# A memory layer with half of its heads multiplied in full: four dense heads and four gathered ones, in 64 slots, with every engine's order planned anew

## The reference

```python
# 1 token mixer: 4 x 4 pixels are pooled into each of 256 tokens by an attention with 8 heads
h1 = mean_of_patch + softmax(q @ k) @ v @ proj_w.T + proj_b
# 2 Mamba-like mixer on layernorm(h1): two selective scans over 256 tokens, 128 channels x 16 states
h2 = h1 + (concat(y_forward * silu(z), y_backward * silu(z)) * gate) @ W_out.T
# 3 product-key memory on layernorm(h2)
q = (x @ Wq_pk).reshape(b, n, 2, 8, 32).transpose(2, 0, 1, 3, 4)
sim = einsum('pbnhd,pkhd->pbnhk', q, pk_keys)      # 2 sides, 8 heads, 64 keys each
scores, idx = top_k(sim, 16)                       # 16 of each side
score = scores[0][..., :, None] + scores[1][..., None, :]
final_scores, pk_idx = top_k(score, 16)            # 16 of the pairs: rows of a table of 4096 per head
weights = softmax(final_scores)
# each token and head: weighted sum of 16 rows of keys_table and values_table,
# then causal attention of each head over the 256 tokens, and Wo
```

## Time and profile before

| | |
|---|---|
| median of 3 runs | 13356.86 us (13354.56 to 13362.06) |
| profiled execution | 13354.71 us, its span 13352.6 us |
| TensorE busy (weight loads) | 11719.0 us, 88% (9286.1 us, 70%) |
| VectorE, ScalarE, POOL busy | 78%, 55%, 77% |
| mean granted TensorE clock | 0.933 |
| indirect DMAs | 9216, 1108 ns each |
| slots | 3584, 56 per image |

### The profile page before, as it was taken

One profiled execution on the slowest core, in us unless ns is written; L12 is line 12 of the kernel. 1 busy time (PEld: TensorE's weight loads), 2 busy tenths in 40 slices (PEclk: granted clock), 3 DMA queues, 4 the chain that ended last, 5 costly groups with the idle time before them and its releaser, 6 DMA issues.

```text
span 13352.6 us, 262103 instructions
## 1 busy us (share of the span) xinstructions
PE 11719.0 (88%) x71396; PEld 9286.1 (70%) x71396; DVE 10428.1 (78%) x39940; ACT 7363.4 (55%) x17030; POOL 10215.8 (77%) x9220
## 2 busy tenths in 40 slices
PE   3888888988989889989889888898888888898988
PEld 3677677776777767777767677776677677776776
DVE  7878778778778787787777877877878878778772
ACT  2555555555555555555555555555555555555554
POOL 1777777777777777777777777777777777777776
PEclk6999999999999999999999999999999999999999
DMA  2555555555555555555555555555555555555554
GB/s 73 160 145 153 157 145 154 154 144 159 145 151 158 144 154 153 147 156 148 149 159 146 151 159 143 155 154 146 157 143 153 159 145 153 158 142 157 152 140 120
DMA packets 1668219, 1983.98 MB, mean 149 GB/s; under 512 B 532846, under 2 KB 1134062, under 8 KB 1666286
## 3 DMA queue, kind: packets, MB, share of 16 engines
q1 hardware_dynamic: 1371566, 1359.71, 35.8%
q0 software_dynamic: 294912, 604.57, 17.5%
HBM read 1898.00 MB, written 65.01 MB: 147 GB/s over the span
## 4 chain that ended last, share of the span: by engine, by line
PE 38%; DVE 26%; POOL 18%; issue 11%; DMA 4%; ACT 2%; SPq 0%; DVEq 0%; POOLq 0%; ACTq 0%
POOL gath L801 18%; PE bank L991 9%; PE bank L1032 6%; PE bank L873 4%; PE bank L1019 3%; DVE apart L1701 3%; PE bank L1006 3%; DVE row_f L1704 3%; DMA gath<-in_table_dram,rowsT 2%; DVE decay L1576 2%; PE bank L954 2%; DVE onehot L1803 2%; PE bank L977 2%; PE bank L1050 1%; DMA moving<-keyspace 1%
## 5 line engine op out<-in xcount | busy, mean ns | idle before, releaser
L801 POOL DMA_INDIRECT gath<-in_table_dram,rowsT x9216 | 10215.6, 1108 | 3105.9 <-issue 2673.7
L1256 ACT ACTIVATE weight<-bank 128x512 f32<-128x512 f32 x3584 | 2139.3, 597 | 4415.0 <-PE bank L1006 4383.9
L991 PE MATMUL bank<-weight,rowtab 128*128 128x256 f32 x12288 | 3373.8, 399 | 0.0
L1032 PEld LDWEIGHTS bank<-spread,gath 128*128 128x128 f32 x18432 | 2519.7, 201 | 727.8 <-DMA gath<-in_table_dram,rowsT 607.6
L1032 PE MATMUL bank<-spread,gath 128*128 128x96 f32 x18432 | 2524.3, 282 | 519.0 <-DMA gath<-in_table_dram,rowsT 518.8
L991 PEld LDWEIGHTS bank<-weight,rowtab 128*128 128x128 f32 x12288 | 2460.7, 202 | 620.3 <-issue 102.2
L1249 ACT ACTIVATE bank<-bank,seventeen 128x512 f32<-128x512 f32 x3584 | 2370.6, 661 | 13.3 <-PE bank L1006 10.2
L1019 PE MATMUL bank<-moving,pick_b 96*128 96x512 bf16 x3584 | 1457.5, 407 | 304.7 <-ACT bank L1249 226.5
L1006 PE MATMUL bank<-moving,pick_b 96*128 96x512 bf16 x3584 | 1435.0, 400 | 71.1 <-DMA moving<-keyspace 70.6
L1568 DVE TENSOR_TENSOR_SCAN decay<-decay,wide 128x1024 f32<-128x1024 f32 x512 | 1169.3, 2285 | 26.4
L1836 DVE SCALAR_TENSOR_TENSOR acc<-bank,rrow,acc 128x64 f32<-128x64 f32 x1024 | 240.5, 276 | 839.3 <-PE bank L1006 797.2
(11 more groups left out here) (268 smaller groups left out, 18929.9 us busy)
## 6 DMA issues: line engine op xcount, KB each, us to landing
rowtab<-in_tableD_dram SPq DMA_DIRECT2D x2048, 256.0 KB
wide<-states SPq DMA_DIRECT2D x512, 512.0 KB
moving<-keyspace SPq DMA_DIRECT2D x3072, 64.0 KB
gath<-in_table_dram,rowsT POOLq DMA_INDIRECT x9216
pix<-in_x_dram SPq DMA_DIRECT2D x504, 256.0 KB
moving<-keyspace SPq DMA_DIRECT2D x3072, 32.0 KB
keyspace<-split SPq DMA_DIRECT2D x192, 256.0 KB, 2.1
moving<-keyhalf SPq DMA_DIRECT2D x512, 64.0 KB
```

Of the source, the lines that this page charges most:

```text
L801: pool.indirect_dma_start(out=gath[:, u % RING, j, :], out_offset=None, in_=table, in_offset=bass.IndirectOffsetOnAxis(ap=rowsT[k][:, col: ...
L991: mm(dense_ps[:, 0:TOK], rowtab[:, r, s % 2 * 2 + half, :], weight[s % 2][:, half * TOK:(half + 1) * TOK], start=(s % 16 == 0 and half == ...
L1032: mm(sums_ps[:, col:col + STREAM], gath[:, u % RING, j, :], flat[:, col:col + STREAM], start=True, stop=True)
L1256: ins = af(weight[s % 2][:], zd_ps[s % 2][:], ACT.Exp, scale=-1.0)
```

## The change

Head 3 becomes dense for all its tokens, and heads 4 to 7 are gathered. The image has 64 full slots in place of 48 full and 8 half ones, 128 gathers in 32 parts in place of 144 in 36, and eight `S.R` in place of ten. The ring of gathered parts has 4 places in place of 6. The table tiles stay 32 per image, the key rows go from 56 loads to 64. The second logarithm `l2`, `selh`, `X5`, `wb4`, `k4` and `K3`'s half go; `split_h` and `keyhalf` are replaced by a fourth full set in `split` and `keyspace`. VectorE's `L` lists work on 8 units in place of 6 and its `G` lists on 8 in place of 10. All four order strings are written anew. `pr0` and `A0` now wait for the `T` lists.

```diff
-DENSE = 3
+DENSE = 4
-HU = DU + TILES
+HU = DU
-SLOTS = 16 * DENSE + 8
+SLOTS = 16 * DENSE
-PARTS = (GH * SPAN - SPAN // 2) // PART
-RING = 6
+PARTS = GH * SPAN // PART
+RING = 4
...
 PE_ORDER = """
...
-21 z20+0 a0.6+0 o21+0 d19+0 g1.5+0 a1.0+0
-22 z21+0 o22+0 d20+0
...
-55 z54+0 o55+0 d53+0 S.E2+1 F.y+2
+1 z0+0 d63-1 o1+0 g0.0+0 a5.6-1 S.A3+0 F.g+1
...
+25 z24+0 o25+0 d23+0 g1.4+0 a0.6+0
+26 z25+0 o26+0 d24+0 a1.0+0
...
+39 z38+0 o39+0 d37+0 g2.3+0 a2.5+0 F.xd+2 F.dt+2
+40 z39+0 o40+0 d38+0
+41 z40+0 o41+0 d39+0 g2.4+0 a2.6+0 S.E0+1
+42 z41+0 o42+0 d40+0 a3.0+0
...
+63 z62+0 o63+0 d61+0 g3.7+0 a5.5+0 S.E2+1 F.y+2
...
 ACT_ORDER = """
...
+0 w63-1 l0+0 k3-1 a5.5-1 F.sq2+2 F.sq3+2 S.E2+0
...
 DVE_ORDER = """
...
+5 a6.3-1 S.n0+1 S.n1+1 S.lo3+0 S.R7+0
...
+40 S.e0+1 S.pr1+1
+41 S.e1+1
+42 F.dl+2 a2.5+0 S.R0+1 a2.6+0
+43 S.e2+1 S.e3+1 F.B0+2
+44 
+45 S.R1+1 F.sf0+2
+46 S.R2+1 a3.3+0
+47 F.sb0+2 F.B1+2 S.lo1+1
+48 F.sf1+2
+49 F.sb1+2 a3.5+0
+50 F.B2+2 a3.6+0 S.e4+1
+51 F.sf2+2 F.C0+2
+52 
+53 F.sb2+2 a4.3+0 F.B3+2
+54 F.C1+2 F.sf3+2
+55 a4.5+0 F.sb3+2
+56 a4.6+0 S.A2+1
+57 F.C2+2 S.wh+1 S.re2+1
+58 S.A3+1 F.C3+2
+59 S.R3+1 a5.3+0
+60 
+61 S.wb0+1 S.e5+1 a5.5+0
+62 S.R4+1 S.lo2+1 S.R5+1
+63 S.wb1+1 S.R6+1
...
 SP_ORDER = """
...
-35 bc+2 m38+0
...
-42 lq0+2 t23+0 m45+0
-43 m46+0
-44 lq1+2 t24+0 m47+0
...
+16 t10+0 x0+3 m19+0
...
+37 x1+3 m40+0
...
+40 t22+0 bc+2 m43+0
...
+48 t26+0 x2+3 m51+0
+49 m52+0
+50 lq1+2 lq0+2 t27+0 m53+0
+51 m54+0
+52 t28+0 st0+1 m55+0
+53 m56+0
+54 x3+3 t29+0 m57+0
+55 m58+0
+56 lq2+2 t30+0 m59+0
+57 m60+0
+58 x4+3 x5+3 st1+1 t31+0 lq3+2 m61+0
+59 x6+3 m62+0
...
+64 x7+3
...
-                if h < DENSE:
-                    mm(dense_ps[:, 0:TOK], rowtab[:, r, s % 2 * 2 + half, :],
...
-                else:
-                    for q in (2 * half, 2 * half + 1):
-                        mm(dense_ps[:, 0:P], rowtab[:, r, q, :], weight[s % 2][:, q * P:(q + 1) * P],
-                           start=(s % 16 == 0 and q == 0), stop=(s == SLOTS - 1 and q == 3),
-                           skip_group_check=True)
+                mm(dense_ps[:, 0:TOK], rowtab[:, r, s % 2 * 2 + half, :],
+                   weight[s % 2][:, half * TOK:(half + 1) * TOK],
+                   start=(s % 16 == 0 and half == 0), stop=(s % 16 == 15 and half == 1),
+                   skip_group_check=True)
```

More of the change, by code:

```diff
@@ L195 @@
+45 w44+0 l45+0 F.dc2+2
+46 w45+0 l46+0 a3.4+0
+47 w46+0 l47+0 F.dc3+2
+48 w47+0 l48+0 k2+0 F.dc4+2 a3.5+0 K2+0
+49 w48+0 l49+0
+50 w49+0 l50+0 F.dc5+2 S.E1+1
+51 w50+0 l51+0 a4.0+0
+52 w51+0 l52+0 S.wg+1
+53 w52+0 l53+0 F.dc6+2
+54 w53+0 l54+0 F.dc7+2
+55 w54+0 a4.4+0 l55+0
+56 w55+0 a4.5+0 l56+0
+57 w56+0 l57+0
+58 w57+0 l58+0 S.hi2+1
+59 w58+0 l59+0 a5.0+0
+60 w59+0 l60+0
+61 w60+0 l61+0
+62 w61+0 l62+0 a5.4+0
+63 w62+0 l63+0 S.mi2+1
 """
 DVE_ORDER = """
-0 a5.6-1 F.y+1 F.ps+2
-1 S.R9+0 S.e6+0
@@ L249 @@
[L249 to L253, removed]
+0 F.y+1 a5.6-1
+1 F.ps+2 F.g+1
+2 S.e6+0 S.e7+0
+3 F.h2+1 S.re3+0
+4
+5 a6.3-1 S.n0+1 S.n1+1 S.lo3+0 S.R7+0
+6 F.rf+2 a6.5-1
+7 a6.6-1 S.T0+1
+8
+9
+10 S.T1+1 S.T2+1 S.T3+1
+11 S.T5+1 S.T4+1
+12
+13 S.T6+1 S.T7+1 a7.3-1
+14 S.T10+1
+15 S.T8+1 S.T9+1 F.var+2 S.wb2+0
+16 S.T11+1 S.T12+1
+17 S.T13+1 a7.5-1
+18 a7.6-1 F.nw0+2 S.T15+1
+19 F.q0+2
+20
+21 a0.3+0 F.q1+2
+22 a0.5+0 S.T16+1
+23 F.q2+2 S.T14+1 F.pv0+2
@@ new lines @@
+24 a0.6+0
+25 S.T17+1
+26 S.cp+1 F.pv1+2 S.T18+1 S.A0+1
+27 F.pv2+2 a1.3+0 S.pr0+1
+28
+29 S.wb3+0 S.L0+1 F.h1+2 S.L1+1
+30 S.L2+1 F.nw1+2 S.L3+1
+31 a1.5+0 S.sel+1 S.wd+1
+32 a1.6+0
+33 S.G0+1 S.wx+1 S.G1+1 S.A1+1
+34 S.G2+1
+35 F.uz0+2 S.G3+1 S.re0+1
+36
+37 S.T19+1 F.uz1+2 S.G4+1
+38 a2.3+0 S.wg+1
+39 S.lo0+1 S.i+1 S.re1+1
+40 S.e0+1 S.pr1+1
[8 more added lines that the diff above has]
+49 F.sb1+2 a3.5+0
@@ L291 @@
 34 t19+0 m37+0
-35 bc+2 m38+0
+35 m38+0
 36 t20+0 m39+0
-37 m40+0
+37 x1+3 m40+0
 38 t21+0 m41+0
 39 m42+0
-40 st0+1 t22+0 m43+0
-41 st1+1 m44+0
-42 lq0+2 t23+0 m45+0
+40 t22+0 bc+2 m43+0
+41 m44+0
+42 t23+0 m45+0
 43 m46+0
-44 lq1+2 t24+0 m47+0
[L302 to L312, removed]
+44 t24+0 st3+0 m47+0
+45 m48+0
+46 t25+0 m49+0
+47 m50+0
+48 t26+0 x2+3 m51+0
[10 more added lines that the diff above has]
+59 x6+3 m62+0
+60 t0+1 m63+0
+61 m0+1
+62 t1+1 m1+1
+63 m2+1
+64 x7+3
 """
@@ L1670, in second @@
                                        for u in range(DU)], (0, 2, 3, 5)[what])
-                if name == "X5":
-                    done("G")
-                    done("Gi")
-                    mark["X"] = lists([(pair[:, DU + u, :], pair[:, DU + u, :], fin[:, DU + u, :], None)
-                                       for u in range(TILES)], 5)
                 if name == "wg":
@@ L1695, in second @@
                         done("pr1")
-                    for other in ("sel", "selh"):
-                        if other in mark:
-                            after(mark[other])
+                    if "sel" in mark:
+                        done("sel")
                     if "R" in mark:
@@ L1725, in second @@
                     mark["i"] = step(v.tensor_copy(idx_b[:], best_i[:, :, 0:HU, :]))
-                if name in ("sel", "selh"):
-                    lo, hi = (0, DU) if name == "sel" else (DU, HU)
-                    for other in ("L" if name == "sel" else "X",):
-                        if other in mark:
-                            after(mark[other])
+                if name == "sel":
+                    lo, hi = 0, DU
+                    if "L" in mark:
+                        done("L")
                     if "R" in mark:
@@ L1788, in second @@
                     side, t = n // 2, n % 2
-                    for other in ("i", "sel", "selh"):
+                    for other in ("i", "sel"):
                         if other in mark:
```

404 lines of the change are left out of this document (152 added, 252 removed).

## The result

The changed kernel takes 12637.81 us (median of 4 runs, 12626.59 to 12655.92) against 13355.71 us for the kernel before, run beside it (4 runs). The ratio is 0.9463, with a 95% interval of 0.9447 to 0.948: 5.4% faster, where 3.1% was forecast. The profiled execution has a span of 12640.9 us and a mean granted clock of 0.973.

A forecast was written before the change was run, and what follows sets the result against it. POOL's gather queue was taken to set the period of 204.5 us per image, with TensorE second. The terms summed to -6.5 us per image, 416 us over 64 images, from 13354.7 to 12940 us; range 12440 to 13300.

The forecast's parts named there:

- likeliest case: Whole kernel: the change goes as forecast, period 195 to 201 us, 12750 to 13160 us, chance 0.55.
- rivals 1 and 2: Whole kernel: 1, as forecast, period 195 to 201 us, chance 0.55; 2, most other waits go too, 190.6 us, 0.18.
- TensorE's work (before the clock): TensorE: 16 full slots added, 8 half slots and 4 parts dropped, +6.9 us per image.
- Clock: Second stage: half-clock time beside two gather waits, 11 us, costs half as much; -5.5 us per image, between 0 and -8.3.
- Waits beside the gathers: TensorE's waits for VectorE: half of the accumulation's 3.6 us goes (-1.8), the one-hot's 2.5 us stays.
- Rival 2: New order also removes most other waits, 7 us left: period 190.6 us, 12465 us, chance 0.18.
- Bare slots: Slots with only z, o and d: TensorE waits 0.44 us for the Relu, 8 such slots for 4; +1.8 us per image.
- Key rows: TensorE's waits for key-row loads, 1.1 us per image, taken to stay unchanged.
- Rival 4: SP's transfer queue: key rows arrive late in rows 41, 50, 56 and 58, +12 us per image, 13707 us; chance 0.12.
- The way by stages: Second sum: slots 0 to 39 take 123.7 us, slots 40 to 63 about 75, 198.7 us per image in all.
- the sign of failure: Slots 40 to 63: the forecast fails if this late stage lasts over 80 us.
- The rule against it: TensorE: skill's weight-load share and MFU give room at 70%, so added slots cost nothing; sum 6.9 us lower.

The follow-up runs named there:

- the run with 108 gathers: Kernel before, three of each four sets gathered (108 per image), TensorE's products kept: 14561 and 14558 us, ratios 0.8374 and 0.8384.

## Why the prediction was right, and where it was off

The direction and the mechanism were right: POOL stopped being the bound, the gather waits went, TensorE became the fullest engine. The likeliest case had a period of 195 to 201 us and the time fell below it, at 193.6 us, between rivals 1 and 2. Term by term, per image:

| term | forecast | measured |
|---|---|---|
| TensorE's work (before the clock) | +6.9 | +7.1 |
| half clock given back | -5.5 | -8.1 |
| gather waits | -7.9 | -7.9 |
| accumulation waits | -1.8 | -3.6 |
| one-hot waits | 0 | -2.5 |
| Relu waits | +1.8 | +2.8 |
| key rows | 0 | +2.9 |
| other short waits | 0 | -1.6 |
| sum | -6.5 | -10.9 |

The waits are those of the stretch, divided by its images. The clock term is counted in the traces: of an image 24.5 us are at half clock before and 7.2 after, and TensorE is busy for 22.2 and 5.9 us of these; half of the 16.3 us between them comes back. The work term is what is then left of TensorE's busy time (182.2 to 181.2). The last row but one is what makes up the fall of all idle time, 22.3 to 12.4. 64 x 10.9 is 698 us, and the span fell by 711.7.

- **Clock: the term that was mis-sized most among those I had.** I put 11 us of half clock down to the two gather waits of the second stage, and left nothing for any other wait. If each stretch at half clock in the trace before is put down to TensorE's longest wait in it or shortly before it, the gathers have 11 to 12.6 us of the 24.5, the accumulation has 7.0 and the one-hot 2.5. So the gathers' share was about right. The other two waits went as well, and their half clock with them: -8.1 in place of -5.5, near my lower bound of -8.3. After the change 5.7 of the 7.2 us that are left sit beside the wait of `o43`, and 1.6 beside a wait of 2.7 us for `z63` that comes in every second image and has no cause in the profile.
- **Waits beside the gathers.** I took half of the accumulation's and none of the one-hot's, reasoning that VectorE and TensorE are near each other in load late in the image. They are (70.7 and 71.1 us in the late stage shown above), but these two waits are gone. That the new order does it, by the slots that it puts between producer and user, is my reading of the order strings; no run takes these entries back one by one. Rival 2 was right in this: with the other short waits, 5.9 us went that my sum had left standing. The Relu and the key rows took back 3.9 us more than my sum had for them, so that 12.4 us of idle time stay where rival 2 left 7.
- **Bare slots.** Right in kind: slots 16, 22, 24, 32, 40, 46, 48 and 54 each lose 0.44 to 0.99 us to the Relu; 1.0 us per image more than I gave it.
- **Key rows.** Rival 4 had the place (the rows of SP after `bc`) and named four crowded rows. Only `m43` behind `bc` cost time, 4.0 us of waiting per image in place of 1.1, under the 6.5 us from which it decides. I took "three slots ahead" as enough for all of them and didn't set `bc`'s own waits, for `xd` and for its store, and the 2 MB of its quarters (the load behind them took 8.94 us to land) against the lead of the one load directly behind it.
- **The way by stages** reached nearly the same sum with two wrong parts: forecast 123.7 and 75 us, measured 113.8 and 79.8 over 55 images (before: 119.6 and 84.9). I had put all relief into the late stage. Over the same images the early stage has TensorE's added work (+1.9 us where I had +2.7) but loses 3.8 us of idle time and 3.9 us through the clock, with the accumulation's waits that the kernel before has in its slots 21 and 28; the late stage keeps 9.3 us of idle time and 70.5 us of busy TensorE, where my 75 us held 7 and 68. The late stage of one image even lasts 82.6 us, over the 80 that was to be the sign of failure. The agreement of the two sums was no confirmation.
- **The rule against it** (the Trainium skill, Perfetto Trace Analysis, Identifying the Most-Contended Engine): by its weight-load share of 70% the added slots would have cost nothing. The trace speaks against that reading: TensorE's work grew by 7.1 us where the start-to-start distances gave 6.9, and at a share of 72% TensorE is busy for 94% of the stretch. No run on an undisturbed chip isolates what these 7 us cost, and the other number that the section names, MFU, was not worked out.
- **A slip in a bound.** A period of 201 us is 13354.7 - 64 x 3.5 = 13131 us; the 13160 of the likeliest case belongs to 201.5. Nothing hangs on it.

That POOL was the bound of the kernel before is what both traces show and what the run with 108 gathers supports, though on chips that charge for gathers in a second way, which that run can't tell from the queue. How much of the 5.4% is due to fewer gathers and how much to the order could be split only there (7.7 and 4.0 of 11.7), and that split doesn't carry over to 13356 us.

## What to carry to other kernels

Take a queue engine's pauses into its load before you call it free: 77% busy was 99% full here. When the bound goes, look at every wait of the second engine that the same edit moves, not only at those for the bound, and look behind each long one for a stretch at half clock. In an ordered queue, put a load with a near due time ahead of a chain that waits for something itself; here that one swap is worth 0.6 to 0.8% on the chips where it was timed. And before you explain "issue" or "remote", count the semaphore events of the trace; a gap before an instruction that waits for nothing is the safe sign of a stopped engine.

## What the hardware showed that I had not expected

- On some chips the same program takes 30% longer (17373 against 13356 us), with the same duration of the exponential (596 and 597 ns). VectorE stops between short instructions that wait for nothing (709 times in 11000 us, never on the undisturbed chip), and the time grows by 1.0 to 1.3 us with every indirect DMA of 128 rows. The cause is open. The kernel before, with 144 per image, loses 30%, the changed one, with 128, 21%.
- On such a chip the rank of what to improve is another: 7.0 us of TensorE's work per image are worth nothing there.
- One wait of 5.19 us was followed by five microseconds at a granted clock of 0.50, in which instructions took 1.91 us in place of 1.03.
